# A distance-weighted graph layer: the reciprocal of every eighth block made by GpSimd in turns 1 to 4, with six weight slots and two late slots

## The chip, the cores and the metric

One Trainium2 chip, one of its cores. The metric is the device time of one execution in microseconds (us), lower is better. Each kernel is also run once under the hardware profiler, and all the rows below come from that one execution.

## What is computed

Two graph layers over the same 4096 x 4096 matrix `adj`, with 128 features, all in fp32:

```python
h = relu(layernorm(x))                     # 4096 x 128
msg = h @ W0 + B0
weights = where(adj < 1, exp(-2 * (1/adj - 1)**2), 0)
x = x + weights @ msg
h = relu(layernorm(x))
A = adj + I;  d = sum(A, axis=1) ** -0.5
x = x + relu((d[:, None] * A * d[None, :]) @ (h @ W1.T))
```

The second layer needs the rows of x that the first one has finished, and both read all of `adj` (64 MB).

## The kernel before

**Tiles.** `adj` is cut into 8 x 8 blocks of 512 x 512. A *turn* g handles the eight blocks of block row g, so there are 64 *units* u = 8g + idx; `ORDER` says in which order the blocks of a row come, and the blocks are loaded in pairs (`raw`, three pair slots). For each unit the kernel makes a 128 x 2048 tile:

- VectorE transposes the block out of `raw` into one of four `kept` slots (`turn`, L661) and makes the cut copy in one of five `wt` slots (`cut`, L676: the value where it is below 1, else 0). From turn 3 on it also sums the rows of a pair (`row_sum`, L669).
- ScalarE turns the cut copy into the weight in place: `log` (L542), `invert` (L547, exp of minus the log, so 1/r), `square` (L552), `weigh` (L561, exp of -2 times it). In turns 0 to 2 VectorE does the square of every fourth or every second unit instead (`quad`, L682), and the last step is L558. The loop of unit u issues log(u), square(u-1), invert(u), weigh(u-1).
- TensorE multiplies the weight tile with `msg` and adds it up over the turn in the bank `acc0` (`multiply_weights`, L392), two units behind (`LAG`). It also multiplies the plain blocks with the second layer's `support`: at once out of `kept` where the support rows exist already (`mix_once`, L405), else later, from a copy that SyncE has spilled to HBM (`spill`, L305) and that GpSimd's queue loads again into one of three `late` slots (L360), or at the end into halves of `raw` (`mix_late`, L415). `JOBS` names the unit whose place each late job has. In turns 0 to 2 TensorE also sums the rows (`sum_tiles`, L423).

**Between turns** one chain makes the support rows of the turn before: ScalarE copies the finished sum (`copy_x1t`, L587), TensorE transposes it (`turn_x1`, L446), VectorE adds x and takes the layer norm (`make_x1`, L758 to L776), TensorE transposes (`turn_hid`, L452), ScalarE copies (`copy_hid`, L599), TensorE multiplies (`multiply_support`, L458), VectorE scales (`make_support`, L787). `STEPS` puts each of these at an idx of the next turn; up to turn 4 `copy_x1t` stands at idx 1, `copy_hid` at 3, `turn_hid` at 4 and `multiply_support` at 5. In TensorE's loop of unit u the steps `turn_hid` and `multiply_support` stand ahead of multiply_weights(u-2).

**Order.** Everything is written by hand: each engine executes its own list in order and waits on semaphores. GpSimd makes the layer-norm input of three quarters of the rows during turn 0 (L345) and after that only issues the loads of `LOADED`, one after another; a load waits until its slot's last job is done (`late_done`) and its block is spilled.

Of the kernel before, what the change touches and what calls it, by code (L numbers as in the profile page):

```python
# [22 lines left out]
T = 4  # L23
RAW, KEPT, WTS, LATE = 3, 4, 5, 3
LAG = 2
# [67 lines left out]


def dve_squares(u):
    return sum(squared_by_dve(v) for v in range(u + 1))


def act_squares(u):
    return sum(not squared_by_dve(v) for v in range(u + 1))  # L100

# [14 lines left out]
def slot_before(j):  # L116

    return max((i for i in range(j) if late_slot(i) == late_slot(j)), default=None)


# [5 lines left out]
def build(nc, x, adj, w0, b0, w1, out):  # L126
# [6 lines left out]
    with ctx:  # L133
# [29 lines left out]
        hid_t = sb("hid_t", [D, ROWS])  # L163
        bn = sb("bn", [P, 8, 6])
        mv = sb("mv", [P, NT, 2])
        var0 = sb("var0", [P, NT])
# [37 lines left out]
        ident_zeroed = sem("ident_zeroed")  # L204
        ident_done = sem("ident_done")
        ones_done = sem("ones_done")
        quads_done = sem("quads_done")
# [18 lines left out]
        ln_done = sem("ln_done")  # L226
        inv_done = sem("inv_done")
        square_done = sem("square_done")
        quad_done = sem("quad_done")
# [103 lines left out]
        def _(pool):  # L333
            nc.gpsimd.memset(ident[:], 0.0).then_inc(ident_zeroed, 1)
            nc.gpsimd.memset(ones_row, 1.0)
            nc.gpsimd.memset(ones[:], 1.0)
            nc.gpsimd.memset(thirty_second[:], 1.0 / B).then_inc(ones_done, 1)
            pool.wait_ge(ident_zeroed, 1)
# [9 lines left out]

            for j, (r, c) in enumerate(LOADED):
# [12 lines left out]

        @block.tensor
        def _(pe):
# [18 lines left out]

            def multiply_weights(u):
                first, last = u % G == 0, u % G == G - 1
                pe.wait_ge(wt_done, u + 1)
# [151 lines left out]
        def _(act):  # L538
# [5 lines left out]
            def invert(u):  # L544
                v = wt[:, u % WTS]
                act.wait_ge(ln_done, u + 1)
                nc.scalar.activation(v, v, ACT.Exp, scale=-1.0).then_inc(inv_done, 1)  # L547

            def square(u):
                v = wt[:, u % WTS]  # L550
                act.wait_ge(inv_done, u + 1)
                nc.scalar.activation(v, v, ACT.Square, bias=-1.0).then_inc(square_done, 1)  # L552

            def weigh(u):
# [4 lines left out]
                else:  # L559
                    act.wait_ge(square_done, act_squares(u))  # L560
                    nc.scalar.activation(v, v, ACT.Exp, scale=-2.0).then_inc(wt_done, 1)  # L561
# [49 lines left out]
            for u in range(UNITS):  # L611
                g, idx = u // G, u % G
                log(u)
                if u >= 1 and not squared_by_dve(u - 1):
                    square(u - 1)
                invert(u)
                if step_at(g, idx, "copy_x1t"):
                    copy_x1t(g - 1)
                if u >= 1:
                    weigh(u - 1)  # L620
                if g == 0 and idx in (1, 3, 5):
                    std_rows((idx + 1) // 2)
                    copy_h0((idx + 1) // 2)
# [24 lines left out]
        def _(dve):  # L648
            def turn(u):
# [21 lines left out]
            def cut(u):  # L671
                v = kept[:, u % KEPT]
                dve.wait_ge(turned, u + 1)
                if u >= WTS:
                    dve.wait_ge(acc0_done, u - WTS + 1)
                nc.vector.scalar_tensor_tensor(out=wt[:, u % WTS], in0=v, scalar=CUTOFF, in1=v, op0=ALU.is_lt,  # L676
                                               op1=ALU.mult).then_inc(cut_done, 1)

            def quad(u):
                v = wt[:, u % WTS]  # L680
                dve.wait_ge(inv_done, u + 1)
                nc.vector.scalar_tensor_tensor(out=v, in0=v, scalar=-2.0, in1=v, op0=ALU.add,  # L682
# [191 lines left out]
```

## Time and profile before

| | us |
|---|---|
| three runs | 611.67, 613.0, 613.95 (median 613.0) |
| the profiled execution | 611.06 |
| its span in the trace | 609.3 |
| TensorE busy / VectorE / ScalarE / GpSimd | 524.3 / 480.5 / 469.0 / 41.4 |

The busy times are shares of one span and say nothing of when an engine waits. The time of an execution is 1.8 us more than its span. In the turns of this text, turn 1 is about 79 to 132 us on the trace's clock (by VectorE's transposes), turn 2 to 188, turn 3 to 253, turn 4 to 316; a turn's sum leaves `acc0` some 30 us after the last of its blocks has been transposed, since ScalarE and TensorE run behind.

### The profile page before, as it was taken

The numbers are of one execution on the slowest core, as the hardware profiler recorded it, in microseconds if no ns is written. First come the engines' busy times: TensorE is split into PE (matmuls) and PEld (weight loads), VectorE is DVE, ScalarE is ACT, GpSimd is POOL, SyncE is SP. The second block draws the span as 40 slices with busy tenths as digits, with TensorE's granted clock in tenths as the row PEclk, the third lists the DMA queues.
The fourth block names the chain that finished last, engine by engine and source line by source line (L and its number), as shares of the span: only waits on it lengthen the run. The fifth ranks groups of instructions, "written<-read, shape, count | busy, mean of one in ns | idle before, by whom it ended". The sixth has DMA issues, their size and how long they took to land.

```text
span 609.3 us, 4840 instructions
## 1 busy us (share of the span) xinstructions
PE 524.3 (86%) x1509; PEld 237.8 (39%) x1509; DVE 480.5 (79%) x553; ACT 469.0 (77%) x308; POOL 41.4 (7%) x68
## 2 busy tenths in 40 slices
PE   2369786979799966898599997899999999999994
PEld 1244432424234423343344443344444444445452
DVE  5899878998897899988999749993999959202156
ACT  2398999999997789996999987999499976910010
POOL 0344200000000000000000000000000000111000
PEclk9759898999999998999989998999999999999998
DMA  7999999999999999799959939899498401299122
GB/s 171 221 254 321 322 317 330 318 309 274 361 325 318 276 331 293 216 262 319 287 133 250 230 155 309 217 210 272 160 248 225 113 20 65 80 418 394 73 67 73
DMA packets 93340, 145.19 MB, mean 238 GB/s; under 512 B 10369, under 2 KB 84354, under 8 KB 84354
## 3 DMA queue, kind: packets, MB, share of 16 engines
q1 hardware_dynamic: 88274, 108.17, 65.7%
q0 software_dynamic: 5040, 36.70, 16.4%
q8 instruction: 12, 0.20, 0.1%
q14 instruction: 14, 0.11, 0.1%
HBM read 106.04 MB, written 38.80 MB: 238 GB/s over the span
## 4 chain that ended last, share of the span: by engine, by line
PE 45%; ACT 19%; DVE 14%; SPq 11%; DMA 5%; issue 4%; DVEq 0%
PE acc L392 14%; PE mix L405 14%; PE mix L415 12%; SPq L294 10%; DVE kept L661 6%; ACT wt L561 5%; DMA adj_t_spill<-kept 5%; ACT wt L542 4%; ACT wt L552 4%; ACT wt L547 4%; DVE wt L676 3%; PE acc L415 2%; PE side L415 1%; DVE wt L682 1%; DVE rowpart L669 1%
## 5 line engine op out<-in xcount | busy, mean ns | idle before, releaser
L392 PE MATMUL acc<-wt,msg 128*128 128x512 f32 x512 | 241.8, 616 | 33.9 <-ACT wt L561 30.9
L392 PEld LDWEIGHTS acc<-wt,msg 128*128 128x128 f32 x512 | 96.8, 196 | 163.2 <-issue 115.3
L661 DVE STREAM_TRANSPOSE kept<-raw 128x2048 f32<-128x2048 f32 x64 | 147.5, 2304 | 12.3 <-DMA adj_t_spill<-kept 10.3
L676 DVE SCALAR_TENSOR_TENSOR wt<-kept 128x2048 f32<-128x2048 f32 x64 | 146.4, 2287 | 1.5
L542 ACT ACTIVATE wt<-wt 128x2048 f32<-128x2048 f32 x64 | 121.7, 1902 | 21.9 <-DVE wt L676 21.9
L547 ACT ACTIVATE wt<-wt 128x2048 f32<-128x2048 f32 x64 | 121.5, 1899 | 0.3
L561 ACT ACTIVATE wt<-wt 128x2048 f32<-128x2048 f32 x54 | 102.5, 1899 | 0.0
L552 ACT ACTIVATE wt<-wt 128x2048 f32<-128x2048 f32 x54 | 102.5, 1897 | 0.0
L405 PE MATMUL mix<-kept,support 128*128 128x512 f32 x224 | 100.6, 594 | 1.0 <-ACT mixed L603 1.0
L415 PE MATMUL mix<-late,support 128*128 128x512 f32 x208 | 93.4, 593 | 2.8 <-DVE support L787 2.8
L669 DVE TENSOR_REDUCE rowpart<-raw 128x16 f32<-128x4096 f32 x20 | 87.6, 4378 | 0.0
L405 PEld LDWEIGHTS mix<-kept,support 128*128 128x128 f32 x224 | 41.9, 190 | 52.4 <-issue 52.1
L415 PEld LDWEIGHTS mix<-late,support 128*128 128x128 f32 x208 | 39.3, 190 | 51.9 <-issue 51.9
L360 POOL DMA_DIRECT2D late<-adj_t_spill x26 | 13.9, 535 | 471.8 <-PE mix L415 389.9
L758 DVE TENSOR_TENSOR x<-side,x 128x512 f32<-128x512 f32 x8 | 5.5, 689 | 49.0 <-PE side L446 49.0
L423 PE MATMUL mix<-kept,ones 128*32 128x512 f32 x192 | 27.2, 641 | 10.8 <-DVE kept L661 10.6
L645 ACT COPY kept<-mix 128x512 f32<-128x512 f32 x6 | 3.5, 586 | 29.9 <-PE mix L415 26.6
L599 ACT COPY hid_t<-side 128x512 f32<-128x512 f32 x8 | 4.6, 575 | 28.1 <-PE side L452 28.1
L682 DVE SCALAR_TENSOR_TENSOR wt<-wt 128x2048 f32<-128x2048 f32 x10 | 22.9, 2287 | 3.3 <-ACT wt L547 3.3
L345 POOL TENSOR_SCALAR support<-x,mv 128x128 f32<-128x128 f32 x24 | 21.9, 930 | 40.1 <-DVE mv L701 40.1
L587 ACT COPY x1t<-acc 128x512 f32<-128x512 f32 x8 | 4.6, 578 | 22.4 <-PE acc L392 22.4
L828 DVE TENSOR_TENSOR kept<-mix,support 128x512 f32<-128x512 f32 x6 | 4.1, 690 | 19.2 <-PE mix L504 19.2
(87 smaller groups left out, 264.7 us busy)
## 6 DMA issues: line engine op xcount, KB each, us to landing
raw<-in_adj_dram SPq DMA_DIRECT2D x512, 128.0 KB, 4.8
adj_t_spill<-kept SPq DMA_DIRECT2D x35, 1024.0 KB, 9.6
late<-adj_t_spill POOLq DMA_DIRECT2D x26, 1024.0 KB, 8.4
raw<-adj_t_spill POOLq DMA_DIRECT2D x9, 1024.0 KB, 10.7
x<-in_x_dram SPq DMA_DIRECT2D x32, 64.0 KB, 3.0
out_dram<-kept SPq DMA_DIRECT2D x32, 64.0 KB, 1.8
w_sb<-in_L_gnn_W_dram SPq DMA_DIRECT2D x1, 64.0 KB
late<-in_L_gnn_W_dram SPq DMA_DIRECT2D x1, 64.0 KB
```

The costliest lines, as they stand in the source:

```text
L294: sp.dma_start(raw[q * B:(q + 1) * B, n % RAW, e:e + 4], adj_parts[g // 2, g % 2, col(2 * n) // 2, q, :, e:e + 4]).then_inc(raw_loaded[n % ...
L392: mm = nc.tensor.matmul(acc0[:], msg[:, col(u) * T + k, :], wt[:, u % WTS, k, :], start=(first and k == 0), stop=(last and k == T - 1))
L405: mm = nc.tensor.matmul(once_bank[g][:], support[:, c * T + k, :], kept[:, u % KEPT, k, :], start=(first and k == 0), stop=False)
L415: mm = nc.tensor.matmul(bank[:], support[:, c * T + k, :], late_tile(slot)[:, k, :], start=(start and k == 0), stop=(stop and k == T - 1))
L542: nc.scalar.activation(v, v, ACT.Ln, bias=LN_GUARD).then_inc(ln_done, 1)
L547: nc.scalar.activation(v, v, ACT.Exp, scale=-1.0).then_inc(inv_done, 1)
L552: nc.scalar.activation(v, v, ACT.Square, bias=-1.0).then_inc(square_done, 1)
L561: nc.scalar.activation(v, v, ACT.Exp, scale=-2.0).then_inc(wt_done, 1)
L661: nc.vector.transpose(dst, src).then_inc(turned, 1)
L669: nc.vector.tensor_reduce(dst, src, AX_X, ALU.add).then_inc(summed, 1)
L676: nc.vector.scalar_tensor_tensor(out=wt[:, u % WTS], in0=v, scalar=CUTOFF, in1=v, op0=ALU.is_lt, op1=ALU.mult).then_inc(cut_done, 1)
L682: nc.vector.scalar_tensor_tensor(out=v, in0=v, scalar=-2.0, in1=v, op0=ALU.add, op1=ALU.mult).then_inc(quad_done, 1)
```

## The change

The third unit of each of the turns 1 to 4 (idx 2, that is u = 10, 18, 26, 34) gets its 1/r from GpSimd: a tensor_tensor adds the guard 2^-30 to the cut copy, a second one raises it to the power -1. ScalarE leaves out `log` and `invert` for these units, and issues their `square` and `weigh` three units later, in the loop of u + 3. TensorE takes the weights in the order in which they are finished, `WEIGHED`: 24, 25, 27, 28, 26, 29 and so on. GpSimd's list now has these two instructions between its loads, placed by `load_unit`. `wt` has six slots instead of five, `late` two instead of three. VectorE's `turn` has an added wait on `tiles_summed`, since the reuse of a `wt` slot no longer implies it.

```diff
-RAW, KEPT, WTS, LATE = 3, 4, 5, 3
+RAW, KEPT, WTS, LATE = 3, 4, 6, 2
...
+POOL_TURNS = (1, 2, 3, 4)
+POOL_IDX = 2
+POOL_DELAY = 3
...
+def inverted_by_pool(u):
+    return u // G in POOL_TURNS and u % G == POOL_IDX
...
+def weigh_order():
...
+    for u in range(UNITS):
+        if not inverted_by_pool(u):
+            order.append(u)
+        if u + 1 >= POOL_DELAY and inverted_by_pool(u + 1 - POOL_DELAY):
+            order.append(u + 1 - POOL_DELAY)
...
+def load_unit(j):
+
+    before = slot_before(j)
+    if before is None:
+        return G + 2 + j
+    return [u for u in sorted(JOBS) for _ in JOBS[u]][before] + 1
...
+            def invert(u):
+                v = wt[:, u % WTS].rearrange("p k i -> p (k i)")
+                pool.wait_ge(power_set, 1)
+                pool.wait_ge(cut_done, u + 1)
+                nc.gpsimd.tensor_tensor(v, v, guard[:, 0:1].to_broadcast([P, T * ROWS]),
+                                        ALU.add).then_inc(pool_guarded, 1)
+                pool.wait_ge(pool_guarded, pool_inverts(u))
+                nc.gpsimd.tensor_tensor(v, v, minus_one[:, 0:1].to_broadcast([P, T * ROWS]),
+                                        ALU.pow).then_inc(pool_inv_done, 1)
...
+            for u in range(G, UNITS):
+                for j in range(len(IN_TURN)):
+                    if load_unit(j) == u:
+                        load_late(j)
+                if inverted_by_pool(u):
+                    invert(u)
+            for j in range(len(IN_TURN), len(LOADED)):
+                load_late(j)
...
-                log(u)
-                if u >= 1 and not squared_by_dve(u - 1):
+                pooled = u - POOL_DELAY if u >= POOL_DELAY and inverted_by_pool(u - POOL_DELAY) else None
+                if not inverted_by_pool(u):
+                    log(u)
+                if u >= 1 and not squared_by_dve(u - 1) and not inverted_by_pool(u - 1):
                     square(u - 1)
-                invert(u)
+                if not inverted_by_pool(u):
+                    invert(u)
+                if pooled is not None:
+                    square(pooled)
...
-                if u >= 1:
+                if u >= 1 and not inverted_by_pool(u - 1):
                     weigh(u - 1)
+                if pooled is not None:
+                    weigh(pooled)
...
+                    if v < PE_SUMS * G:
+                        dve.wait_ge(tiles_summed, v + 1)
```

ScalarE's list in turn 3 before, from copy_x1t(2) through weigh(28).

```order
L587 COPY x1t<-acc0 128x512 [waits acc0_done]
L561 ACTIVATE wt<-wt 128x2048 [waits square_done]
L542 ACTIVATE wt<-wt 128x2048 [waits cut_done]
L552 ACTIVATE wt<-wt 128x2048 [waits inv_done]
L547 ACTIVATE wt<-wt 128x2048 [waits ln_done]
L561 ACTIVATE wt<-wt 128x2048 [waits square_done]
```

```order
L591 ACTIVATE inv<-pows 128x8 [waits pows_done]
L599 COPY hid_t<-side 128x512 [waits hid_turned]
L595 ACTIVATE inv<-inv 128x8 [waits pows_ln]
L542 ACTIVATE wt<-wt 128x2048 [waits cut_done]
L552 ACTIVATE wt<-wt 128x2048 [waits inv_done]
```

The first piece is weigh(24) and the loop of unit 26 (log 26, square 25, invert 26, weigh 25); the loop of 27 with the same four rows stands between the pieces, and the second piece goes on with the loop of 28. Now, from copy_x1t(2) on, through the loops of 26 to 29:

```order
L659 COPY x1t<-acc0 128x512 [waits acc0_done]
L633 ACTIVATE wt<-wt 128x2048 [waits square_done]
L624 ACTIVATE wt<-wt 128x2048 [waits inv_done]
L633 ACTIVATE wt<-wt 128x2048 [waits square_done]
L611 ACTIVATE wt<-wt 128x2048 [waits cut_done]
L616 ACTIVATE wt<-wt 128x2048 [waits ln_done]
L663 ACTIVATE inv<-pows 128x8 [waits pows_done]
L671 COPY hid_t<-side 128x512 [waits hid_turned]
L667 ACTIVATE inv<-inv 128x8 [waits pows_ln]
```

```order
L611 ACTIVATE wt<-wt 128x2048 [waits cut_done]
L624 ACTIVATE wt<-wt 128x2048 [waits inv_done]
L616 ACTIVATE wt<-wt 128x2048 [waits ln_done]
L624 ACTIVATE wt<-wt 128x2048 [waits pool_inv_done]
L633 ACTIVATE wt<-wt 128x2048 [waits square_done] x2
```

The loop of 26 is only square(25) and weigh(25), the loop of 27 only log and invert, and the loop of 28 (four rows, not shown) has square(27) and weigh(27). The last piece is the loop of 29: log 29, square 28, invert 29, square 26, weigh 28, weigh 26. So the third weight of the turn, which was that of unit 26 and followed log(27), is now that of unit 27 and follows log(28).

GpSimd's list from the first reload on, before:

```order
L360 DMA late<-adj_t_spill 128x2048 [waits spilled0]
L360 DMA late<-adj_t_spill 128x2048 [waits spilled1]
L360 DMA late<-adj_t_spill 128x2048 [waits spilled2]
L360 DMA late<-adj_t_spill 128x2048 [waits spilled2,late_done]
```

and now, at the same place and once more around the fourth reciprocal:

```order
L419 DMA late<-adj_t_spill 128x2048 [waits spilled0]
L401 TENSOR_TENSOR wt<-wt,guard 128x2048 [waits cut_done,power_set]
L404 TENSOR_TENSOR wt<-wt,minus_one 128x2048 [waits pool_guarded]
L419 DMA late<-adj_t_spill 128x2048 [waits spilled1]
L419 DMA late<-adj_t_spill 128x2048 [waits spilled2,late_done]
L401 TENSOR_TENSOR wt<-wt,guard 128x2048 [waits cut_done,power_set]
```

```order
L419 DMA late<-adj_t_spill 128x2048 [waits spilled1,late_done]
L401 TENSOR_TENSOR wt<-wt,guard 128x2048 [waits cut_done,power_set]
L404 TENSOR_TENSOR wt<-wt,minus_one 128x2048 [waits pool_guarded]
```

The second reload now stands behind the reciprocal of unit 10, the third waits for the first job instead of going out freely, and the reciprocal of unit 34 stands behind the eighth reload, which waits for the job of unit 33.

## Rows read from the trace of the kernel before

**Rows 1.** The page, busy time, share and instructions of each engine.

```profile
PE 524.3 (86%) x1509; PEld 237.8 (39%) x1509; DVE 480.5 (79%) x553; ACT 469.0 (77%) x308; POOL 41.4 (7%) x68
```

**Rows 2.** Busy time by stretch; after the engines the granted clock, DMA share, GB/s.

```profile
152.00:216.00 64.00, 59.07 (x186) 24.59 (x184) 56.64 (x49) 53.03 (x33) 1.06 (x2) 1.00 1.06 317
216.00:280.00 64.00, 52.11 (x125) 23.10 (x125) 61.52 (x48) 59.14 (x37) 1.06 (x2) 0.95 0.96 284
280.00:346.00 66.00, 57.27 (x143) 25.86 (x142) 63.39 (x49) 66.00 (x41) 1.58 (x3) 0.97 0.86 232
346.00:609.00 263.00, 246.04 (x643) 113.31 (x641) 168.27 (x201) 166.75 (x111) 12.61 (x24) 0.99 0.60 184
```

**Rows 3.** The chain that ended last (start, us, what), two pieces.

```profile
146.56 16.12 DMA adj_t_spill<-kept
...
218.45 1.80 ACT wt L542
```

**Rows 4.** Timeline of ScalarE in turn 3 (start, us, engine, line, out<-in).

```profile
218.35 1.90 ACT L542 ACTIVATE wt<-wt 128x2048 f32<-128x2048 f32 x1
...
233.42 1.90 ACT L542 ACTIVATE wt<-wt 128x2048 f32<-128x2048 f32 x1
...
240.62 1.90 ACT L542 ACTIVATE wt<-wt 128x2048 f32<-128x2048 f32 x1
```

**Rows 5.** Timeline of VectorE in turn 3.

```profile
208.40 2.29 DVE L676 SCALAR_TENSOR_TENSOR wt<-kept 128x2048 f32<-128x2048 f32 x1
...
219.24 2.28 DVE L676 SCALAR_TENSOR_TENSOR wt<-kept 128x2048 f32<-128x2048 f32 x1
...
226.74 2.29 DVE L676 SCALAR_TENSOR_TENSOR wt<-kept 128x2048 f32<-128x2048 f32 x1
...
235.47 2.28 DVE L676 SCALAR_TENSOR_TENSOR wt<-kept 128x2048 f32<-128x2048 f32 x1
...
238.53 1.13 DVE L787 TENSOR_SCALAR support<-side,scale 128x128 f32<-128x128 f32 x4
```

**Rows 6.** Timeline of TensorE in turn 3.

```profile
232.90 3.70 PE L392 MATMUL acc<-wt,msg 128*128 128x512 f32 x8 [1.36 <-ACT wt L561]
...
240.77 5.35 PE L392 MATMUL acc<-wt,msg 128*128 128x512 f32 x8 [3.28 <-ACT wt L561]
247.97 3.70 PE L392 MATMUL acc<-wt,msg 128*128 128x512 f32 x8 [1.85 <-ACT wt L561]
...
255.17 3.70 PE L392 MATMUL acc<-wt,msg 128*128 128x512 f32 x8
```

**Rows 7.** Timeline in turn 4: VectorE, then TensorE.

```profile
297.66 2.28 DVE L676 SCALAR_TENSOR_TENSOR wt<-kept 128x2048 f32<-128x2048 f32 x1
...
301.28 1.13 DVE L787 TENSOR_SCALAR support<-side,scale 128x128 f32<-128x128 f32 x4 [0.60 <-PE side L458]
...
304.46 5.40 PE L392 MATMUL acc<-wt,msg 128*128 128x512 f32 x8 [3.29 <-ACT wt L561]
```

**Rows 8.** Timeline in turn 2, VectorE and TensorE.

```profile
165.11 2.29 DVE L676 SCALAR_TENSOR_TENSOR wt<-kept 128x2048 f32<-128x2048 f32 x1
...
167.87 3.70 PE L392 MATMUL acc<-wt,msg 128*128 128x512 f32 x8 [1.67 <-ACT wt L561]
...
171.40 1.05 PE L458 MATMUL side<-w1t,hid_t 128*128 128x128 f32 x8
...
174.94 1.13 DVE L787 TENSOR_SCALAR support<-side,scale 128x128 f32<-128x128 f32 x4
```

**Rows 9.** Timeline of GpSimd: reloads around turns 2 and 4.

```profile
146.58 1.05 POOL L360 DMA_DIRECT2D late<-adj_t_spill x2 [81.89 <-DMA adj_t_spill<-kept]
...
283.43 0.53 POOL L360 DMA_DIRECT2D late<-adj_t_spill x1 [20.29 <-PE mix L415]
```

**Rows 10.** GpSimd's L345 alone (min/median/max ns), and a cut during it.

```profile
L345 POOL TENSOR_SCALAR support<-x,mv x24: 702/712/2472, 24.7 to 62.8; 128x128 f32<-128x128 f32 x24
...
27.02 2.29 DVE L676 SCALAR_TENSOR_TENSOR wt<-kept 128x2048 f32<-128x2048 f32 x1
```

More of the change, by code:

```diff
@@ L92, in step_at, with act_inverts, pool_inverts, square_count @@
     return g >= 1 and idx == STEPS[name][g >= EARLY_TURNS]
+POOL_TURNS = (1, 2, 3, 4)
[4 more added lines that the diff above has]
+def weigh_order():
+    order = []
+    for u in range(UNITS):
[3 more added lines that the diff above has]
+            order.append(u + 1 - POOL_DELAY)
+    return order
+WEIGHED = weigh_order()
+def act_inverts(u):
+    return sum(not inverted_by_pool(v) for v in range(u + 1))
+def pool_inverts(u):
+    return sum(inverted_by_pool(v) for v in range(u + 1))
+def square_count(u):
+    return sum(not squared_by_dve(v) for v in WEIGHED[:WEIGHED.index(u) + 1])
 def dve_squares(u):
     return sum(squared_by_dve(v) for v in range(u + 1))
-def act_squares(u):
-    return sum(not squared_by_dve(v) for v in range(u + 1))
 def first_job(u):
@@ L164, in build @@
         bn = sb("bn", [P, 8, 6])
+        minus_one = sb("minus_one", [P, 1])
+        guard = sb("guard", [P, 1])
         mv = sb("mv", [P, NT, 2])
@@ L205, in build @@
         ident_done = sem("ident_done")
+        power_set = sem("power_set")
         ones_done = sem("ones_done")
@@ L227, in build @@
         inv_done = sem("inv_done")
+        pool_guarded = sem("pool_guarded")
+        pool_inv_done = sem("pool_inv_done")
         square_done = sem("square_done")
@@ L336, in _ @@
             nc.gpsimd.memset(ones[:], 1.0)
+            nc.gpsimd.memset(guard[:], LN_GUARD)
+            nc.gpsimd.memset(minus_one[:], -1.0).then_inc(power_set, 1)
             nc.gpsimd.memset(thirty_second[:], 1.0 / B).then_inc(ones_done, 1)
@@ L347, in _, with load_late @@
                 last.then_inc(h0_done, 1)
-            for j, (r, c) in enumerate(LOADED):
+            def invert(u):
[7 more added lines that the diff above has]
+                                        ALU.pow).then_inc(pool_inv_done, 1)
+            def load_late(j):
+                r, c = LOADED[j]
                 slot = late_slot(j)
@@ L382, in multiply_msg, with multiply_weights @@
                 last.then_inc(m_multiplied, 1)
-            def multiply_weights(u):
-                first, last = u % G == 0, u % G == G - 1
-                pe.wait_ge(wt_done, u + 1)
+            def multiply_weights(n):
+                u = WEIGHED[n]
+                first, last = n % G == 0, n % G == G - 1
+                pe.wait_ge(wt_done, n + 1)
                 if u < G and u % 2 == 0:
@@ L545, in invert @@
                 v = wt[:, u % WTS]
-                act.wait_ge(ln_done, u + 1)
+                act.wait_ge(ln_done, act_inverts(u))
                 nc.scalar.activation(v, v, ACT.Exp, scale=-1.0).then_inc(inv_done, 1)
@@ L550, in square @@
                 v = wt[:, u % WTS]
-                act.wait_ge(inv_done, u + 1)
+                if inverted_by_pool(u):
+                    act.wait_ge(pool_inv_done, pool_inverts(u))
+                else:
+                    act.wait_ge(inv_done, act_inverts(u))
                 nc.scalar.activation(v, v, ACT.Square, bias=-1.0).then_inc(square_done, 1)
@@ L559, in weigh @@
                 else:
-                    act.wait_ge(square_done, act_squares(u))
+                    act.wait_ge(square_done, square_count(u))
                     nc.scalar.activation(v, v, ACT.Exp, scale=-2.0).then_inc(wt_done, 1)
@@ L674, in cut @@
                 if u >= WTS:
-                    dve.wait_ge(acc0_done, u - WTS + 1)
+                    dve.wait_ge(acc0_done, WEIGHED.index(u - WTS) + 1)
                 nc.vector.scalar_tensor_tensor(out=wt[:, u % WTS], in0=v, scalar=CUTOFF, in1=v, op0=ALU.is_lt,
@@ L680, in quad @@
                 v = wt[:, u % WTS]
-                dve.wait_ge(inv_done, u + 1)
+                dve.wait_ge(inv_done, act_inverts(u))
                 nc.vector.scalar_tensor_tensor(out=v, in0=v, scalar=-2.0, in1=v, op0=ALU.add,
```

## Prediction

> **What bounds the kernel now.** I read the page's totals first, then the chain of waits, then the busy times by stretch, then the timelines of turns 2 to 4. The totals show no engine that is full: TensorE 86%, VectorE 79%, ScalarE 77% of the span [rows 1]. So the stage decides. The stretches run from one copy_x1t to the next (turn 3's products fall in 216 to 280, turn 4's in 280 to 346). In 216 to 280 ScalarE is busy 59.1 of 64 us, but VectorE 61.5; in 280 to 346 ScalarE 66.0 of 66 and VectorE 63.4; TensorE has 12 and 9 us of gaps there. From 346 on TensorE is busy 246 of 263 us: what it loses before stays lost, what it gains stays gained [rows 2]. Before 216 the transfers carry 317 GB/s [rows 2], and the chain runs through a spill that takes 16 us to land [rows 3]; after that it runs along ScalarE's unit of four instructions, one each 1.80 us [rows 3].
>
> The reader should see one thing in turn 3: ScalarE is the last link, but VectorE is close ahead of it. The cut of unit 28 ends at 229.0 and its log starts at 233.4, a lead of 4.4 us; for unit 29 it is 237.75 and 240.6, a lead of 2.9 [rows 4, 5]. A ScalarE that has less to do soon stands before a cut that isn't made.
>
> **What leaves ScalarE.** A log and an exp in each of four turns: 8 instructions of 1.80 us [rows 3], 14.4 us in all. The two that are moved, square and weigh, still cost their 3.6 us, three units later. Whether the 14.4 us show at the end hangs on whether TensorE gets its weights earlier.
>
> **What the new order does to TensorE in turn 3.** Before, the third weight of the turn (unit 26) follows log(27). Now the third is unit 27, and its weigh stands behind log(28), so it needs a cut that comes one unit later. The first free moment for log(28) is the end of cut 28, 229.0 [rows 5]. Three more instructions in front of and with the weigh: 229.0 + 3 x 1.8 + 1.9 = 236.3, against 232.9 where the third product started before [rows 6]. The fourth (unit 28) stands behind log(29), which can't start before 237.75 [rows 5], and behind four more instructions, since square(26) is put in there: 237.75 + 4 x 1.8 + 1.9 = 246.9, against 240.8 [rows 6]. From there TensorE is full. The fourth product, 3.5 us, ends at 250.4; the fifth (unit 26, its weight is there at 248.7) starts then, and from the fifth to the sixth it is 7.2 us, a product and a late job, as before (247.97 to 255.17). So the sixth starts at 257.6 instead of 255.2 [rows 6]. That is **+2.4 us**. VectorE sees the same delay: the support rows of turn 2 need multiply_support, which stands behind the third product: 236.3 + 3.5 + 1.0 = 240.8 against 238.5 [rows 5]. I put that at nothing extra, since it is the same delay.
>
> **Turn 4.** Again the fourth weight (unit 36) is the one that counts. It follows log(37), and cut 37 ends at 299.95 [rows 7]; 299.95 + 4 x 1.8 + 1.9 = 309.05, against a product that started at 304.46 and was the last to wait for ScalarE before TensorE runs full [rows 7]. **+4.6 us.** In both turns the weights from the fifth on are earlier by up to 3.6 us, but by then TensorE has a queue of late and at-once products, and it is idle no more.
>
> **Turns 1 and 2 and the late slot.** With two late slots the load for unit 30 can't go out at 146.6 together with the one before it [rows 9]; it waits for the job of unit 22, in the next turn. That takes 1.05 MB out of the stretch in which VectorE waits 16 us for a spill [rows 3]: 1.05 MB at 317 GB/s [rows 2] is 3.3 us, so cut 20 could end 3.3 us early, at 164.1 instead of 167.4 [rows 8]. But here too the third weight (unit 19) now stands behind the log of the next unit, which waits for cut 20 and a small copy, to about 164.8, and behind invert(20): 164.8 + 2 x 1.8 + 1.9 = 170.3, against a product at 167.9 before; 3.5 us of product and 1.0 of multiply_support give 174.9, and make_support started at 174.94 before [rows 8]. The gain is eaten: 0, at best -3.3. Turn 1 has the same shape, 0, with the same bounds of 3 us to both sides.
>
> **What GpSimd adds.** The two instructions are on no row. From below each takes at least what VectorE's cut of the same shape takes, 2.3 us [rows 5], 4.6 together. From above: GpSimd's own L345 takes 0.712 us for 128 columns [rows 10], 16 times as much for 2048 is 11.4, 22.8 together; a power can be dearer still. I take 16 us, nearer to GpSimd's own row than to VectorE's, but with part of the 0.712 us fixed. The tightest place is unit 34: its add stands behind the reload that went out at 283.4 [rows 9], so it starts at 284.0, and the result is asked for behind log(37), square(36) and invert(37), at 299.95 + 5.4 = 305.4. That is 21.4 us, enough for 16; 22.8 would cost 1.4. In turn 3, from the end of cut 26 at 210.7 [rows 5] to 243, there is room for 32. So 0. The Trainium skill (GPSIMD Engine Reference, Performance versus the Vector engine) gives 4.5 us for a tensor_tensor add of 2048 fp32 columns and holds elementwise work to be VectorE's; it has no price for a power, no run here shows either yet, and the sum above does without it.
>
> **What is nothing.** The sixth `wt` slot: VectorE never waited long for a slot, so there is nothing to give back. Two late slots in turns 5 to 7 and at the end: a job's load goes out after the job two before, at least three units (some 20 us) ahead. The reload behind the reciprocal of unit 10 is used a turn later. The added tiles_summed wait asks for a sum that TensorE made four units ago. If that cover were gone, TensorE would wait for a landing.
>
> **Sum.** 611.06 (the profiled execution, 1.76 over its span, and 1.9 under the median of the runs) + 2.4 + 4.6 + 0 + 0 = 618.1; on the scale of the median 613.0 + 7.0 = **620.0**.
>
> **Rivals.** *Forecast* (chance 0.41): as above, 614 to 626.
>
> *The shared port* (0.26). During turn 0 GpSimd's L345 takes 0.71 us each, but 2.47 for the three of 24 that lie under a cut, and the cut itself keeps its 2.29 us [rows 10]: GpSimd was held, VectorE not. Nothing shows what happens when a long GpSimd instruction reads first. If VectorE's cut is then held to its end, then with an add of 5 and a power of 11 us: in turn 3 the power runs until 210.7 + 16 = 226.7, and cut 27, due at 219.2, waits 7.5 us [rows 5]; in turn 4 5 to 11; in turns 1 and 2 some 8, less the 3 of slack. With a power of 5 us it is about 2 in each. Total +8 to +36 over the forecast; the middle gives 640. The Trainium skill (SBUF - State Buffer, Who interferes with whom) says this outright: a VectorE instruction with two SBUF inputs and a GpSimd instruction that reads SBUF exclude each other, and whichever comes second waits for all of the first. By that rule the trace agrees in the one direction it shows; by that rule the time would be this rival's. I don't take it as the likeliest since the other direction is on no row.
>
> *ScalarE's time comes back* (0.17, the faster side). If VectorE runs further ahead in the new kernel, so that cut 29 is done by 231.6 instead of 237.75, the fourth weight is as early as before and the fifth 3.6 us earlier; turns 3 and 4 give 3.6 each and the lighter transfers of turn 2 their 3.3: 613.0 - 10.5 = 602.5; one of them missing, 606. Against it: VectorE is busy 61.5 of 64 us there [rows 2], and nothing in the change takes work from it. For it: its gaps in turns 1 and 2 are waits for transfers, and these get lighter.
>
> *It cancels* (0.13): the 3.3 us of turn 2 survive, and cut 37 comes 3 us early with them: +0.6, 613.6.
>
> *The power is far dearer* (0.03): at 25 us the reciprocal comes 9 us late in turn 4, and 2 to 4 in turns 1 and 2: 633.
>
> **How the numbers follow.** A measurement of this kernel can tell about 0.5%, 3 us, from no change. Faster by more: the third rival, 0.17. Same: the fourth and the forecast's lower edge, 0.13 and 0.04 of the forecast's. Slower: 0.37 + 0.26 + 0.03 = 0.66. The range leaves out about a tenth at each end: 605, where the faster rival is half counted, to 645, which takes in the port rival up to somewhat over its middle.
>
> **What would show it.** Right: ScalarE has gaps before its logs of units 28, 29 and 37, released by VectorE's cut; the third and fourth products of turns 3 and 4 start later than before, turn 3's sixth by 2 to 3 us; copy_x1t(4) is about 7 us late, and everything behind it equally; GpSimd's pair takes under 21 us and no cut is held. Wrong: a cut that starts long after the transpose or row sum before it, with no semaphore named (the port); ScalarE released by GpSimd; copy_x1t(3) well before 280 (then VectorE's lead was larger than I read it).

## The result and the profile after

The changed kernel takes 1909.7 us (median of four runs, 1908.84 to 1910.6) against 613.5 for the kernel before in the same comparison: a ratio of 3.12, with a 95% interval of 3.1107 to 3.1305. The prediction was 620.0, with a range of 605 to 645. It was wrong by a factor, not by a few per cent.

The page of the changed kernel, busy time per engine (answers to [rows 1]), then the chain that ended last, then the costliest groups (line, engine, operation, out<-in, count | busy us, mean ns | idle us before it and its releaser):

```profile
PE 539.2 (28%) x1509; PEld 242.8 (13%) x1509; DVE 1762.3 (92%) x553; ACT 457.9 (24%) x300; POOL 1363.4 (71%) x78
...
DVE wt L757 40%; DVE hid L851 29%; PE acc L461 5%; PE mix L474 4%; PE mix L484 4%; DVE kept L742 2%; ACT wt L611 2%; ACT wt L624 2%; ACT wt L616 2%; ACT wt L633 1%; DVE rowpart L750 1%; PE acc L484 1%; PE side L484 0%; DVE wt L763 0%; SPq L340 0%
...
L404 POOL TENSOR_TENSOR wt<-wt,minus_one 128x2048 f32<-128x2048 f32 x4 | 1307.3, 326819 | 0.3
L757 DVE SCALAR_TENSOR_TENSOR wt<-kept 128x2048 f32<-128x2048 f32 x64 | 867.8, 13560 | 1.5
L851 DVE TENSOR_SCALAR hid<-x,mv 128x128 f32<-128x128 f32 x32 | 563.6, 27382 | 0.3
...
L401 POOL TENSOR_TENSOR wt<-wt,guard 128x2048 f32<-128x2048 f32 x4 | 14.4, 3598 | 48.7 <-DVE wt L757 48.7
```

One power of 128 x 2048 on GpSimd takes 326.8 us, 160 ns for a column; the add of the same shape takes 3.6. Four powers are 1307 us, and the kernel is 1296 us slower. But the chain does not name GpSimd. It names two VectorE lines, the cut (L757, L676 before) and the layer-norm scaling `hid` (L851, L770 before). These do the same work as before: the other 61 cuts still take 2.29 us. VectorE shows as 92% busy although it has no work added.

Where the time sits is read in the timelines of turn 1 (start us, us, engine, line, what, [idle before <-releaser]). GpSimd:

```profile
94.10 3.59 POOL L401 TENSOR_TENSOR wt<-wt,guard 128x2048 f32<-128x2048 f32 x1 [30.02 <-DVE wt L757]
97.77 327.77 POOL L404 TENSOR_TENSOR wt<-wt,minus_one 128x2048 f32<-128x2048 f32 x1
425.52 0.63 POOL L419 DMA_DIRECT2D late<-adj_t_spill  x1
```

VectorE at the same time, then ScalarE:

```profile
95.26 4.58 DVE L763 SCALAR_TENSOR_TENSOR wt<-wt 128x2048 f32<-128x2048 f32 x1 [1.33 <-ACT wt L616]
99.77 0.15 DVE L825 COPY pows<-side 128x4 f32<-128x4 f32 x1
99.95 2.31 DVE L742 STREAM_TRANSPOSE kept<-raw 128x2048 f32<-128x2048 f32 x1
102.30 244.51 DVE L757 SCALAR_TENSOR_TENSOR wt<-kept 128x2048 f32<-128x2048 f32 x1
346.73 0.68 DVE L839 TENSOR_TENSOR x<-side,x 128x512 f32<-128x512 f32 x1
347.44 0.88 DVE L843 BATCH_NORM_STATS2 bn<-x 128x6 f32<-128x128 f32 x4
348.35 0.38 DVE L847 BATCH_NORM_AGGREGATE mv<-bn 128x2 f32<-128x6 f32 x4
348.76 77.41 DVE L851 TENSOR_SCALAR hid<-x,mv 128x128 f32<-128x128 f32 x4
426.00 0.18 DVE L856 TENSOR_SCALAR pows<-pows 128x4 f32<-128x4 f32 x1
```

```profile
346.83 1.91 ACT L611 ACTIVATE wt<-wt 128x2048 f32<-128x2048 f32 x1 [245.05 <-DVE wt L757]
...
439.37 1.89 ACT L624 ACTIVATE wt<-wt 128x2048 f32<-128x2048 f32 x1
441.16 1.89 ACT L616 ACTIVATE wt<-wt 128x2048 f32<-128x2048 f32 x1
442.96 1.89 ACT L624 ACTIVATE wt<-wt 128x2048 f32<-128x2048 f32 x1
```

Three things are to be seen. The cut and the four `hid` instructions are not idle: they are long, with no wait and no semaphore in front of them. They lie beside a GpSimd instruction that reads and writes SBUF, the on-chip memory, and no semaphore stands in front: this points to the prediction's rival of a shared port, in which one engine has to wait for the other's access. A transpose, a small copy and the statistics run at their usual length in between. And the log on ScalarE is released by the cut, 245 us late, while the square that needs GpSimd's result (442.96) has no wait in front of it: GpSimd's result was there at 425.5, before anything could ask for it. In the three turns after it the picture is the same, except that in turn 4 the cut comes before the power and the `hid` step takes the whole of it (328.07 us).

The excess of the two lines over their busy time without the power (146.4 and 7.0 us in the run e1 below) is 721.4 + 556.6 = 1278 us. The rest of the difference, some 18 us, is about what the new order costs by itself (15.9 us in e1). So there were two questions: what makes the 1278 us, and whether the port is the only thing that would; and what the change is worth when GpSimd costs nothing.

### The profile page after: what moved, and what is told of

The parts are those of the page before. It is cut to its first block, busy times and chain, and to the rows that moved or that the text cites. A ratio compares the mean times of both kernels' runs of the same rounds, so it can differ in the third digit from the quotient of the medians.

```text
span 1908.0 us, 4855 instructions
## 1 busy us (share of the span) xinstructions
PE 539.2 (28%) x1509; PEld 242.8 (13%) x1509; DVE 1762.3 (92%) x553; ACT 457.9 (24%) x300; POOL 1363.4 (71%) x78
## 4 chain that ended last, share of the span: by engine, by line
DVE 74%; PE 16%; ACT 7%; issue 2%; SPq 1%; DMA 0%; DVEq 0%
DVE wt L757 40%; DVE hid L851 29%; PE acc L461 5%; PE mix L474 4%; PE mix L484 4%; DVE kept L742 2%; ACT wt L611 2%; ACT wt L624 2%; ACT wt L616 2%; ACT wt L633 1%; DVE rowpart L750 1%; PE acc L484 1%; PE side L484 0%; DVE wt L763 0%; SPq L340 0%
## 5 line engine op out<-in xcount | busy, mean ns | idle before, releaser
L404 POOL TENSOR_TENSOR wt<-wt,minus_one 128x2048 f32<-128x2048 f32 x4 | 1307.3, 326819 | 0.3
L757 DVE SCALAR_TENSOR_TENSOR wt<-kept 128x2048 f32<-128x2048 f32 x64 | 867.8, 13560 | 1.5
L851 DVE TENSOR_SCALAR hid<-x,mv 128x128 f32<-128x128 f32 x32 | 563.6, 27382 | 0.3
L521 PE MATMUL side<-ident,hid 128*128 128x128 f32 x32 | 6.9, 354 | 1266.7 <-DVE hid L851 1266.7
L611 ACT ACTIVATE wt<-wt 128x2048 f32<-128x2048 f32 x60 | 114.3, 1904 | 769.5 <-DVE wt L757 769.5
L461 PE MATMUL acc<-wt,msg 128*128 128x512 f32 x512 | 251.8, 638 | 52.5 <-ACT wt L633 40.3
L521 PEld LDWEIGHTS side<-ident,hid 128*128 128x128 f32 x32 | 4.9, 178 | 1272.1 <-DVE hid L851 1270.0
L461 PEld LDWEIGHTS acc<-wt,msg 128*128 128x128 f32 x512 | 101.3, 204 | 189.6 <-issue 125.7
L616 ACT ACTIVATE wt<-wt 128x2048 f32<-128x2048 f32 x60 | 113.9, 1899 | 0.4
L624 ACT ACTIVATE wt<-wt 128x2048 f32<-128x2048 f32 x54 | 102.4, 1896 | 0.0
L633 ACT ACTIVATE wt<-wt 128x2048 f32<-128x2048 f32 x54 | 102.1, 1898 | 0.1
L484 PE MATMUL mix<-late,support 128*128 128x512 f32 x192 | 86.2, 592 | 1.8 <-DVE support L868 1.8
L401 POOL TENSOR_TENSOR wt<-wt,guard 128x2048 f32<-128x2048 f32 x4 | 14.4, 3598 | 48.7 <-DVE wt L757 48.7
```

Source lines behind the costliest of these rows:

```text
L404: nc.gpsimd.tensor_tensor(v, v, minus_one[:, 0:1].to_broadcast([P, T * ROWS]), ALU.pow).then_inc(pool_inv_done, 1)
L484: mm = nc.tensor.matmul(bank[:], support[:, c * T + k, :], late_tile(slot)[:, k, :], start=(start and k == 0), stop=(stop and k == T - 1))
L611: nc.scalar.activation(v, v, ACT.Ln, bias=LN_GUARD).then_inc(ln_done, 1)
L851: last = nc.vector.tensor_scalar(hid[:, a, :], x1[:, g * T + a, :], mv1[:, a, 0:1], 0.0, ALU.subtract, ALU.max)
```

## The experiments

The theory after the result: the power's length does it, through the shared port. The rival: the port is only where it shows, and a result that comes 330 us late, or GpSimd's queue behind it, would cost as much by itself. Each run is compared with runs of the kernel before on the same chip (medians 612.3 to 612.4 us).

### e1: the order alone

```diff
-                nc.gpsimd.tensor_tensor(v, v, guard[:, 0:1].to_broadcast([P, T * ROWS]),
+                nc.gpsimd.tensor_tensor(v[:, 0:8], v[:, 0:8], guard[:, 0:1].to_broadcast([P, 8]),
...
-                nc.gpsimd.tensor_tensor(v, v, minus_one[:, 0:1].to_broadcast([P, T * ROWS]),
-                                        ALU.pow).then_inc(pool_inv_done, 1)
+                nc.gpsimd.tensor_tensor(v[:, 0:8], v[:, 0:8], guard[:, 0:1].to_broadcast([P, 8]),
+                                        ALU.add).then_inc(pool_inv_done, 1)
```

> Both GpSimd instructions shrunk to 8 columns (an add of the guard each), so ScalarE gets a tile that has not been inverted; the order on ScalarE and TensorE, the slots and GpSimd's list are those of the change. This is the change with GpSimd's work at nearly no cost. Order theory (my forecast): 618 to 621 us, the fourth product of turn 3 at 246.9 instead of 240.8. Theory that ScalarE's 14.4 us come back: 602 to 606. If neither: 613.

Measured: 628.2 us, ratio 1.0276 (1.0247 to 1.0304), 15.9 us over the kernel before and outside all three ranges of the expectation. The change is slower even when GpSimd's work costs nothing, and by more than the forecast's 7 us. TensorE's products of turn 2, the third and the fourth, and VectorE's wait there for the support rows (they answer to [rows 8]), then turn 3's third and fourth product (they answer to [rows 6]):

```profile
174.63 5.83 PE L461 MATMUL acc<-wt,msg 128*128 128x512 f32 x8 [6.23 <-ACT wt L630]
184.83 5.40 PE L461 MATMUL acc<-wt,msg 128*128 128x512 f32 x8 [2.49 <-ACT wt L633]
...
181.46 1.13 DVE L868 TENSOR_SCALAR support<-side,scale 128x128 f32<-128x128 f32 x4 [5.07 <-PE side L527]
...
248.26 6.55 PE L461 MATMUL acc<-wt,msg 128*128 128x512 f32 x8 [10.05 <-ACT wt L633]
...
258.78 3.70 PE L461 MATMUL acc<-wt,msg 128*128 128x512 f32 x8 [3.08 <-ACT wt L633]
```

The starts of copy_x1t, from ScalarE's timelines of four kernels, show in which turn time is lost (us; e10 and e11 come below):

| copy_x1t of turn | 0 | 1 | 2 | 3 | 4 |
|---|---|---|---|---|---|
| before | 95.50 | 152.68 | 216.05 | 279.74 | 345.71 |
| e1, order of the change | 95.43 | 156.19 | 227.88 | 293.64 | 361.94 |
| e10, only turns 3 and 4 | 96.67 | 153.27 | 216.03 | 281.79 | 350.08 |
| e11, joined one unit later | 95.24 | 150.36 | 211.88 | 275.26 | 338.06 |

Turn 1 loses 3.6 us in e1, turn 2 8.3, turn 3 2.1 and turn 4 2.3; after that nothing more.

### e2: the slots alone

```diff
-RAW, KEPT, WTS, LATE = 3, 4, 5, 3
+RAW, KEPT, WTS, LATE = 3, 4, 6, 2
...
+                    if v < PE_SUMS * G:
+                        dve.wait_ge(tiles_summed, v + 1)
```

> The kernel before with six weight slots and two late slots and nothing else. Order theory: the slots cost nothing and take 1 MB out of turn 2: 610 to 613.5 us. If two late slots starve TensorE: above 616, with TensorE waiting for a reload.

Measured: 612.9 us, ratio 1.0007 (0.9987 to 1.0026). No effect. In turn 2 the transfers do carry less (276 GB/s in the stretch 153 to 216 against 319 before), but nothing comes of it.

### e3 and e4: GpSimd instructions of ordinary length

e3 makes the power a multiplication by -1 of full width, e4 keeps the power on 96 of the 2048 columns:

```diff
-                                        ALU.pow).then_inc(pool_inv_done, 1)
+                                        ALU.mult).then_inc(pool_inv_done, 1)
```

```diff
-                nc.gpsimd.tensor_tensor(v, v, minus_one[:, 0:1].to_broadcast([P, T * ROWS]),
+                nc.gpsimd.tensor_tensor(v[:, 0:96], v[:, 0:96], minus_one[:, 0:1].to_broadcast([P, 96]),
```

> The power becomes a multiplication by -1 over the full 2048 columns (so the tile is not inverted); all else as the change. An add of this size took 3.6 us in the changed kernel, so the pair is about 7.2 us per turn. Port theory: VectorE's two-input instructions are held up to 3.6 us by each, 3 to 10 us over e1. No port: the same as e1.

> The power over 96 of the 2048 columns only (the others stay not inverted), 96 x 160 ns = 15.3 us by the changed kernel's 327 us for 2048; with the add 19 us, about what I had assumed for the whole pair. Late-result theory: the result is there before ScalarE asks for it, so the same as e1. Port theory: a cut or a hid instruction is held some 10 to 15 us in each of four turns: 30 to 50 us over e1.

Measured: e3 640.2 us, ratio 1.0459 (1.043 to 1.0487); e4 635.3 us, ratio 1.0381 (1.0354 to 1.0408). In e3 the multiplication takes 3.60 us alone and 5.53 where a quad of VectorE runs into its start, a cut goes up to 3.16 us, a quad up to 4.07 and a `hid` up to 3.62: each holds the other, for a few us. e3 is 12 us over e1; that is what two GpSimd instructions of 3.6 us per turn cost here on top of the new order. What makes it so much was not taken apart: in the old order the same add and a short power cost nothing (e6 below). e4's power takes 16.6 us (15.6 to 17.6), just what the prediction had assumed for the pair. One line's durations over the whole e4 (min/median/max ns) and a cut that lies wholly inside a power of e4 (158.31 to 175.89):

```profile
L757 DVE SCALAR_TENSOR_TENSOR wt<-kept x64: 2273/2291/2295, 19.9 to 539.4; 128x2048 f32<-128x2048 f32 x64
...
158.31 17.58 POOL L404 TENSOR_TENSOR wt<-wt,minus_one 128x96 f32<-128x96 f32 x1
...
162.84 2.29 DVE L757 SCALAR_TENSOR_TENSOR wt<-kept 128x2048 f32<-128x2048 f32 x1
```

No cut was held by that power at all. So VectorE is not simply locked out for as long as the GpSimd instruction lasts. Neither branch of e4's expectation came: 7 us over e1, not 0 and not 30 to 50. These 7 us were not taken apart: its full-width adds hold quads (up to 4.82 us), and its weights come 20 us later.

### e5 and e6: GpSimd's work on a tile that nobody uses

The kernel before with two late slots, with its own order and ScalarE's full work; GpSimd does the add and the power at the same places, on a tile of its own, 2048 columns in e5 and 96 in e6. Nobody waits for the result.

```diff
-POOL_TURNS = (1, 2, 3, 4)
+POOL_TURNS = ()
+SPARE_TURNS = (1, 2, 3, 4)
...
-                v = wt[:, u % WTS].rearrange("p k i -> p (k i)")
+                v = spare
```

> Order, ScalarE's work and TensorE's are those of the kernel before (five weight slots, two late slots); GpSimd does its add and its power over 2048 columns in the same four turns, but on a tile of its own that nobody reads or waits for. Port theory: VectorE is held by the power all the same, 4 x about 320 us: 1850 to 1920 us. Late-result theory (ScalarE waits for a slow result): 610 to 616 us.

> As the run with the power on a tile of its own, but 96 columns of power (15 us) per turn. Port theory: 635 to 665 us. Late-result theory: 610 to 616 us.

Measured: e5 1885.1 us (one run), e6 612.3, ratio 1.0003 (0.9982 to 1.0023). In e5 GpSimd and VectorE look as in the changed kernel:

```profile
97.76 327.77 POOL L409 TENSOR_TENSOR spare<-spare,minus_one 128x2048 f32<-128x2048 f32 x1
...
102.28 244.51 DVE L762 SCALAR_TENSOR_TENSOR wt<-kept 128x2048 f32<-128x2048 f32 x1
...
348.75 77.42 DVE L856 TENSOR_SCALAR hid<-x,mv 128x128 f32<-128x128 f32 x4
```

A power whose result is never read costs all but 25 us of the whole, so no wait for its result is needed. GpSimd's reloads of `late` are as late here as in the changed kernel, but TensorE stands before its late products for 1.4 us in all, and for `support`, not for a reload (changed kernel: 1.8). The held VectorE instructions are enough by themselves. e6 shows the other side: four adds and four powers of 16.6 us on GpSimd, in the old order, cost nothing that can be measured.

### e7: the power in four instructions of 512 columns

```diff
-                nc.gpsimd.tensor_tensor(v, v, minus_one[:, 0:1].to_broadcast([P, T * ROWS]),
-                                        ALU.pow).then_inc(pool_inv_done, 1)
+                for k in range(4):
+                    s = v[:, k * 512:(k + 1) * 512]
+                    last = nc.gpsimd.tensor_tensor(s, s, minus_one[:, 0:1].to_broadcast([P, 512]), ALU.pow)
+                last.then_inc(pool_inv_done, 1)
```

> The change with the power in four instructions of 512 columns, one behind the other, same work in all. If the port is held for one instruction: VectorE gets a two-input instruction in between the pieces, each held at most about 80 us instead of 245, and the time falls by the units that get through meanwhile, 20 to 30 us per turn: 1800 to 1870 us. If GpSimd keeps the port as long as it has instructions, or if the late result alone sets the time: 1900 to 1915 us.

Measured: 1845.3 us (one run). GpSimd works as long as before, but VectorE runs freely: its longest cut is 3.15 us (by the add) and its longest `hid` 2.03. GpSimd's timeline, VectorE's and ScalarE's:

```profile
101.40 329.56 POOL L406 TENSOR_TENSOR wt<-wt,minus_one 128x512 f32<-128x512 f32 x4
...
105.42 0.88 DVE L853 TENSOR_SCALAR hid<-x,mv 128x128 f32<-128x128 f32 x4
...
108.70 2.29 DVE L759 SCALAR_TENSOR_TENSOR wt<-kept 128x2048 f32<-128x2048 f32 x1
...
431.00 1.91 ACT L626 ACTIVATE wt<-wt 128x2048 f32<-128x2048 f32 x1 [307.71 <-POOL wt L406]
```

and the waits (who <- for whom: us in total, times, longest us):

```profile
ACT wt L626 <- POOL wt L406: 1208.5, 4, 307.7
```

Now it is the late result: ScalarE stands some 300 us before the pooled square in every turn, 308 in the longest. TensorE waits for no reload here either. So the rival is right too: with VectorE free the time is nearly the same. In the changed kernel the held VectorE hides this wait, since it stands still for as long. The time lies in the expectation's first range, but by luck: no cut was held between the pieces, and it is the late result, the reason given for the other range, that sets it.

### e8: both taken away

The split power on GpSimd's own tile: no VectorE instruction held for long, no result waited for.

```diff
-                v = wt[:, u % WTS].rearrange("p k i -> p (k i)")
+                v = spare
...
+                for k in range(4):
+                    s = v[:, k * 512:(k + 1) * 512]
+                    last = nc.gpsimd.tensor_tensor(s, s, minus_one[:, 0:1].to_broadcast([P, 512]), ALU.pow)
```

> The power on GpSimd's own tile again (nobody waits for it), now in four instructions of 512 columns, which in the run with the split power held no cut for long. GpSimd works the same 327 us per turn. If the port is what cost 1270 us in the run with the whole power on its own tile: 610 to 620 us here. If GpSimd's load on the core costs time by itself (or its late reloads do): well above 640.

Measured: 1713.1 us, ratio 2.797 (2.788 to 2.8067). The 610 to 620 us of the port theory missed; the other branch named the late reloads. GpSimd's list is executed in order, and the reloads of `late` stand behind the powers; then TensorE:

```profile
101.31 330.98 POOL L411 TENSOR_TENSOR spare<-spare,minus_one 128x512 f32<-128x512 f32 x4
432.25 1.16 POOL L426 DMA_DIRECT2D late<-adj_t_spill  x2
433.42 3.61 POOL L406 TENSOR_TENSOR spare<-spare,guard 128x2048 f32<-128x2048 f32 x1
...
437.31 2.93 PE L491 MATMUL mix<-late,support 128*128 128x512 f32 x3 [251.04 <-DMA late<-adj_t_spill]
```

```profile
PEld mix L491 <- DMA late<-adj_t_spill: 1101.3, 4, 302.3
```

There is a third way to the same loss: a reload that is issued 300 us late. The 1100 us that it adds are the four waits of the last row.

### e9: one power of 1024 columns, on the spare tile

```diff
-                nc.gpsimd.tensor_tensor(v, v, minus_one[:, 0:1].to_broadcast([P, T * ROWS]),
+                nc.gpsimd.tensor_tensor(v[:, 0:1024], v[:, 0:1024], minus_one[:, 0:1].to_broadcast([P, 1024]),
```

> The power on GpSimd's own tile, one instruction of 1024 columns, some 164 us. If GpSimd works in pieces of 512 columns and keeps the read side of the port until it has read the last piece, and the write side to the end: the first cut is held to half of it (about 80 us after its start), the hid instruction to the end (another 80), and the time is 613 + 4 x about 155 = 1200 to 1250 us. If a cut is always held to three quarters, it ends at 123 us. If the whole is one lock, the first cut is held for all 160 us.

Measured: 1238.5 us (one run). Turn 3, GpSimd and VectorE:

```profile
529.67 163.24 POOL L409 TENSOR_TENSOR spare<-spare,minus_one 128x1024 f32<-128x1024 f32 x1
...
534.37 79.81 DVE L762 SCALAR_TENSOR_TENSOR wt<-kept 128x2048 f32<-128x2048 f32 x1
```

The cut ends at 614.18; less its own 2.29 it was let in at 611.9, 82.2 us after the power began, half of its 163.2. Turn 2 gives the same (84.2 of 165.2). In turn 1 the cut got in before the power, and the `hid` step took the whole of it, 161.8 us. In the changed kernel it was let in at 102.30 + 244.51 - 2.29 = 344.5, 246.8 us into a power of 327.8, three quarters. In e7 and e4, with 512 and 96 columns, it was not held. All of these fit one picture, inferred and not shown: GpSimd takes such an instruction in pieces of 512 columns (some 82 us each), and a cut is let in as soon as the last piece has been read. `hid`, with one input and one output in SBUF, is held to the end of a power of 1024 or 2048 columns (to 426.0 in the changed kernel, against a power that ends at 425.5) and not at all by one of 512. No row names the pieces. Why a power of one piece doesn't hold `hid` is open.

### e10: the order, in turns 3 and 4 only

```diff
-POOL_TURNS = (1, 2, 3, 4)
+POOL_TURNS = (3, 4)
```

(on top of e1's edit)

> As the run with the shrunk GpSimd instructions (628.2 us), but only in turns 3 and 4. My working gave turn 3 +2.4, turn 4 +4.6 and turns 1 and 2 nothing: that makes 618 to 620. By the copies of the sum in that run's trace turns 1 and 2 made 11.9 of its 16.2 us, turns 3 and 4 4.4: 615.5 to 618.

Measured: 616.4 us, ratio 1.0078 (1.0051 to 1.0106), over 12 runs. By the table above turn 3 loses 2.07 us and turn 4 2.32, 4.4 together: turns 3 and 4 cost by themselves what they cost in e1.

### e11: joined one unit later

```diff
-POOL_DELAY = 3
+POOL_DELAY = 1
```

(on top of e1's edit: the weights are finished in the old order, and ScalarE only lacks the log and exp of four units)

> As the run with the shrunk GpSimd instructions, but joined one unit later instead of three, so that the order of the weights is the natural one; ScalarE is still without log and exp of four units, 14.4 us less. Order theory: the loss is gone; what ScalarE's relief is worth by itself shows here, 600 to 611 us. If the relief itself or GpSimd's list cost the time: 625 to 630 as before.

Measured: 603.7 us, ratio 0.986 (0.9833 to 0.9886): 8.6 us faster than before. ScalarE's 14.4 us are worth 8.6 if the order is left alone, and the order of the change costs 628.2 - 603.7 = 24.5 us against that. Turn 3's third and fourth product, with a copy_x1t at 211.88:

```profile
225.55 5.40 PE L461 MATMUL acc<-wt,msg 128*128 128x512 f32 x8 [3.35 <-ACT wt L633]
233.43 3.70 PE L461 MATMUL acc<-wt,msg 128*128 128x512 f32 x8 [1.59 <-ACT wt L633]
```

They start 13.7 and 21.6 us after the copy. Before it was 16.9 and 24.7, in e1 20.4 and 30.9. This kernel doesn't make the four units' reciprocals, so it is a bound and no version to use.

### e12: the reciprocal on VectorE

The old order, no GpSimd; VectorE inverts the four units.

```diff
+                dve.wait_ge(cut_done, u + 1)
+                nc.vector.tensor_scalar(v, v, LN_GUARD, None, ALU.add).then_inc(dve_guarded, 1)
+                dve.wait_ge(dve_guarded, dve_inverts(u))
+                nc.vector.reciprocal(v, v).then_inc(dve_inv_done, 1)
...
-                log(u)
+                if not inverted_by_dve(u):
+                    log(u)
```

> The third unit of turns 1 to 4 is inverted by VectorE itself (the guard added by a tensor_scalar, then a reciprocal instruction, both 128x2048), at the place where ScalarE took it in the kernel before; nothing on GpSimd is added, and the unit is not put off. The relief of ScalarE is that of e11_tiny_delay1 (-8.6 us against before). If a reciprocal of 128x2048 costs about what a cut does (2.3 us), the four units add 4 x some 3.4 us to VectorE, part of it beside ScalarE: 603 to 613 us. If it costs several times a cut (some 17 us), VectorE becomes the bound and the kernel takes 650 to 680 us.

Measured: 653.3 us, ratio 1.0656 (1.0617 to 1.0694). VectorE in turn 1:

```profile
97.08 1.23 DVE L702 TENSOR_SCALAR wt<-wt 128x2048 f32<-128x2048 f32 x1
98.34 12.95 DVE L704 RECIPROCAL wt<-wt 128x2048 f32<-128x2048 f32 x1
```

A reciprocal takes 12.95 us, 5.7 cuts, and of the 4 x 14.2 us put on VectorE 49.5 show at the end against e11. ScalarE's log and exp take 3.6 us for the same tile, so neither VectorE's reciprocal nor GpSimd's power is a cheap 1/r here. A division on GpSimd was not tried. No version was found that beats the kernel before.

## Why the prediction was wrong

**What GpSimd adds: this step failed.** It took 16 us for the pair, from L345's 0.712 us for 128 columns, with 22.8 as the upper bound. The pair takes 3.6 + 326.8 = 330.4 us. The add lies between the bounds, well toward the lower one, and under the 4.5 us quoted in the prediction for it. The power is 29 times the 11.4 us that the step allowed it. L345 is a multiply and an add per element, so its row bounds a multiply and an add; it says nothing of a power, and the text saw that ("a power can be dearer still") and still let 22.8 close the range. The row was used for a shape when what was unknown was the operation. The step's "So 0" also let the pair run beside VectorE for nothing. In its place the runs show 1278 us of held VectorE instructions in the changed kernel, and about as much in e5, where no one waits for the result.

With the measured price, the step's own arithmetic would have come close in size, by another path. It found 21.4 us of room in turn 4 and 32 in turn 3. At 330 us the result is late by 298 to 309 in these turns, some 1210 us if all four are alike, against the 1208.5 us of waiting in e7. In the changed kernel itself ScalarE never waits for the power.

**What leaves ScalarE: right in amount, and it shows.** The prediction left open whether the 14.4 us reach the end. Alone they are worth 8.6 us (e11). The forecast's wording, that the weights from the fifth on are earlier but meet a full TensorE, holds for the order of the change; in the old order the third and fourth gain as well.

**The new order in turn 3: right.** The third product was to start 3.4 us later and the fourth 6.1; against the turn's copy_x1t they are 3.5 and 6.2 later in e1. The sixth and the turn were to be 2.4 late; they are 2.2 and 2.1.

**Turn 4: right in kind, half in size.** The fourth product was to be 4.6 late and is 4.7 (323.04 against 304.46, with copies at 293.64 and 279.74). But it takes 3.70 us where it took 5.40 [rows 7], since TensorE's granted clock was 1.00 there and 0.68 before, and 2.3 us remain of the 4.6 at the turn's end.

**Turns 1 and 2: wrong, 0 instead of 3.6 and 8.3.** This is a second step that failed, small beside the first. The sum let a cut 20 that is 3.3 us earlier pay for the later third weight, and stopped at the third product. Both halves are off. First, VectorE does not wait 16 us for a spill in that stretch: 16.12 us is what the transfer takes on the chain [rows 3], and VectorE stands still for 1.76 of them (the row at 162.77), so 3.3 us were not to be had. In e1 cut 20 starts 10.4 us after the turn's copy against 12.4 before, 2.0 earlier. Second, it is the fourth product that counts, as in turns 3 and 4. Turn 2 before, then ScalarE's log of unit 21 in e1 and the cut that it waits for:

```profile
162.77 2.31 DVE L661 STREAM_TRANSPOSE kept<-raw 128x2048 f32<-128x2048 f32 x1 [1.76 <-DMA adj_t_spill<-kept]
...
174.09 3.70 PE L392 MATMUL acc<-wt,msg 128*128 128x512 f32 x8 [0.63 <-ACT wt L558]
```

```profile
173.35 2.29 DVE L757 SCALAR_TENSOR_TENSOR wt<-kept 128x2048 f32<-128x2048 f32 x1
...
175.67 1.91 ACT L611 ACTIVATE wt<-wt 128x2048 f32<-128x2048 f32 x1 [1.10 <-DVE wt L757]
```

By the prediction's own rule the fourth weight of e1 is ready four more instructions behind that cut: 175.64 + 4 x 1.8 + 1.9 = 184.7, and its product starts at 184.83. Against the turn's copy that is 28.6 us where it was 21.4, 7.2 later, and it takes 5.40 us instead of 3.70; the fifth product and the turn are 8.3 late. In turn 1 the fourth product is 7.9 late in the same way, and the products behind it, which follow closer in e1, take back all but the 3.6.

The third product of turn 2 starts 3.3 us later after the copy, and takes 5.83 us instead of 3.70 after TensorE had stood still for 6.2 us: its granted clock was 0.63 in the product's stretch (174.6 to 180.4), between the two levels of 1.2 and 2.4 GHz, and 1.00 in the same product before. The support rows are late by both, and VectorE waits for them 5.4 us in turn 1, 5.1 in turn 2 (the row at 181.46), 5.5 in turn 3 and 5.9 in turn 4, against 0.6 at most before. The prediction put this at nothing extra. The wait does not decide what a turn loses: it is about the same in all four, the turns lose 3.6, 8.3, 2.1 and 2.3, and cut 21 above is made ahead of it.

**What is nothing: right for the slots** (e2), and the added wait with them. "The reload behind the reciprocal of unit 10 is used a turn later" was right only for a reciprocal of ordinary length; e8 shows what it hides, 1100 us.

**The rivals.** *The shared port* is right as a mechanism, with a power priced at 11 us. The sign that the text gave for it shows in another form: the held cut does not start late, it starts at once and lasts 244.5 us, with no semaphore in front. At the price that the text assumed, a power of 96 columns holds no cut (e4); the 635.3 us of e4 lie in this rival's span of 628 to 656 by luck, for the new order makes 15.9 us of its loss. That it is a port of SBUF is the reading of the page named next; the traces show who is held, and until when. The Trainium skill (SBUF - State Buffer, Who interferes with whom) says that whichever of the two comes second waits for all of the first. The trace agrees that a two-input VectorE instruction waits for GpSimd's, and that transposes and row sums don't; it doesn't agree with "all of the first": the cut was let in after three quarters of 2048 columns and half of 1024, and not held by 512 or fewer. *ScalarE's time comes back* is right as a term (e11) but not the end of the sum. *Far dearer* had the right direction of the price, at 25 us, but another path: ScalarE waiting for the result, which happens in e7 and not in the changed kernel.

**Sum of what was measured.** 612.3 (before) - 8.6 (ScalarE relieved, e11) + 24.5 (order, e1) + 1278 (VectorE held) = 1906, against 1909.7. The two middle terms together are e1's 15.9.

## What to carry to other kernels

An operation that no row shows on that engine has no upper bound from rows of other operations; leave the range open at the top, or measure one instruction first. A very long instruction on a helper engine costs through several doors, the port, its result and its queue. Here closing one of them, or even two, changed little: 1910 us with all open, 1885 without the result (e5), 1845 without the port (e7), 1713 with the queue alone (e8). Before work is taken off an engine, see that the order of the rest can stay: here the relief was worth 8.6 us and the putting off cost 24.5.

## What the runs showed that was not expected

- GpSimd's elementwise power in fp32 takes 16.6 us for 96 columns, 82 for 512, 163 to 165 for 1024 and 326.8 for 2048: about 160 ns a column, 91 times the add (3.6 us).
- GpSimd's power over 1024 or 2048 columns holds a VectorE instruction with two SBUF inputs only until its last 512 columns begin, by the times of the release, and one that scales a tile from SBUF to SBUF to its end; over 512 columns or fewer it holds neither. Splitting it at 512 columns frees VectorE and leaves GpSimd's time at 328 to 331 us a tile (e5 against e8: the held 245 and 77 us are gone).
- The time of a held instruction counts as VectorE's busy time: 92% busy is a wait here, and only the longest of a line's durations (244507 ns against a median of 2292) shows it.
- VectorE's reciprocal of 128 x 2048 takes 12.95 us, 5.7 times a cut.
